# Moving per-head and closing arithmetic of a two-layer graph attention kernel from VectorE to GpSimd

## The chip, the core and the metric

The kernel runs on one core of a Trainium2 chip. The metric is the device time of one execution in microseconds (us). The core has five engines that run their own instruction streams and meet only in semaphores: TensorE (PE in the profile; its weight loads are listed apart as PEld), VectorE (DVE), ScalarE (ACT), GpSimd (POOL) and SyncE (SP, which here only issues DMAs). Kernels are compared by the median of several executions of each on the same chip.

## What is computed

Two graph attention layers over 4096 nodes with 128 features, each followed by a residual sum and a layernorm. `adj` is a 4096 x 4096 matrix of 0 and 1. Layer 0 has four heads of width 32, layer 1 has one head of width 128:

```python
# layer 0, for each head h (W: 128x128, a: 1x4x64)
Wh = (h @ W).reshape(N, H, D)
s_src = jnp.einsum('nhd,hd->nh', Wh, a_src)
s_dst = jnp.einsum('nhd,hd->nh', Wh, a_dst)
e = s_src[:, None, :] + s_dst[None, :, :]
e = jnp.where(e >= 0, e, ALPHA * e)
e = jnp.where(adj[:, :, None] > 0, e, NEG_INF)
attention = jax.nn.softmax(e, axis=1)
h_prime = jnp.einsum('ijh,jhd->ihd', attention, Wh)
return jax.nn.elu(h_prime.reshape(N, H * D))
# around the layers
x = _layernorm(x + _L0_gnn_ref(x, adj, L0_gnn_W, L0_gnn_a), axis=-1)
x = _layernorm(x + _L1_gnn_ref(x, adj, L1_gnn_a), axis=-1)
```

Layer 1 does the same with one head on a logarithmic map of the rows, and maps its result back.

## The kernel before, in words

The exponential of a leaky ReLU of a sum falls into two products, one for pairs whose sum is positive ("above") and one for the others ("below"). So a head is two matrix products of 0/1 masks with weighted values, and the masks are all that depends on the pair. This is what the engines do for layer 0:

- The 4096 target rows are cut into four chunks (`NC` = 4, counter `c`) of 1024 columns. A chunk has four heads, a head eight units, so `U` = 32 units per chunk (counter `u`, `UH` = 8 per head). A unit covers four source tiles of 128 nodes.
- A unit's comparison is made by ScalarE (four `Sign` activations, L620) or by VectorE (four `tensor_scalar`, L633), as the table `ON_ACT` says, letter A or V. VectorE then ANDs it with the adjacency mask (L653 after ScalarE, L657 after itself), which gives the "below" mask. A unit marked `-` in the table `DIRECT` gets a second VectorE instruction, an XOR (L663), for the "above" mask. A unit marked D has no XOR: TensorE multiplies the whole adjacency mask instead, with the below mask taking part in both column groups, so its 64 matmuls (L688) are 32 of 99 columns and 32 of 198 columns, against 64 of 99.
- Masks pass to TensorE through `ring`: six slots for below masks and two for above masks. VectorE waits before an XOR until an above slot is free.
- After a head, `take_head` sums the four accumulator banks out of PSUM (L704, four `tensor_reduce`; they free the banks for the next head) and then does the head's arithmetic in SBUF: scale by `lift` (L708), subtract (L709), reciprocal (L712), divide (L713). It stands behind unit `u % 8 == 1` of the next head (`TAKE_AT` = 1).
- After a chunk's last head, ScalarE takes an exponential for the ELU (`elu_exp`, L721, at u = 4 of the next chunk), and VectorE closes the chunk in five pieces behind units 3, 4, 5, 6 and 11 (`PIECES_AT`): `hidden_sum` (L466, L468), `moments` (L473), `centre` (L479 to L482), and two times `dot` (multiply L488 and row sum L489).
- Meanwhile TensorE transposes the next chunk's adjacency (L536), eight transposes to a group and sixteen groups to a chunk, ScalarE takes them (L543), and GpSimd issues the loads of adjacency tiles (`load_adj`, L501). Issuing DMAs is all that GpSimd does from 9 us on.
- In the last chunk VectorE and ScalarE also begin with layer 1: square roots, logarithms and exponentials of the rows that are already closed, then its weighted values (L731 to L752).
- Layer 1 then runs over eight runs of 512 rows (matmuls L1277, L1299, L1289), with the comparisons on ScalarE (L767).

The order of every engine's work is written out by hand: each engine has its own loop over `c` and `u`, and what stands behind which unit is given by numbers such as `TAKE_AT`.

## Time and profile before

| | us |
|---|---|
| median of 3 runs | 916.73 (915.87 to 918.69) |
| the profiled execution, its own time | 914.89 |
| its span, first to last instruction | 913.1 |
| PE busy | 839.0 |
| DVE busy | 761.4 |
| ACT busy | 694.4 |
| POOL busy | 43.0 |

Busy time is the time in which an engine works on at least one instruction; loads, waits and semaphore instructions are not in it. The granted TensorE clock over the span is 0.976 of full speed. Layer 0's units run from about 77 us to 541 us, layer 1's matmuls from 580 us to the end. In the chain of work that ended last, TensorE has 50% of the span, ScalarE 24% and VectorE 18%.

### The profile page before, as it was taken

How to read it: one execution, taken by the hardware profiler on the slowest of the kernel's cores; microseconds unless marked ns; L12 is line 12 of the kernel's file. 1: busy time of each engine (PE TensorE's matmuls, PEld its weight loads, DVE VectorE, ACT ScalarE, POOL GpSimd, SP SyncE). 2: the span in 40 equal slices, each digit the busy share in tenths (PEclk: the TensorE clock that was granted, in tenths of full speed). 3: DMA queues.
4: the chain of work that ended last, by engine and by line, in shares of the span. 5: the costliest groups of instructions: out<-in, count | busy, mean ns of one | idle time of the engine just before them, and what ended most of it. 6: DMA issues, size and time to landing. Idle time of an engine off the chain costs nothing.

```text
span 913.1 us, 24394 instructions
## 1 busy us (share of the span) xinstructions
PE 839.0 (92%) x10868; PEld 686.8 (75%) x10868; DVE 761.4 (83%) x1306; ACT 694.4 (76%) x815; POOL 43.0 (5%) x80
## 2 busy tenths in 40 slices
PE   8496999989999889999998898599999999999995
PEld 6496999978999879999998884355555555555552
DVE  3978889899988999889997889775877786878876
ACT  3999998897999989999986994968373654637222
POOL 3200000000000000000000000000000100000000
PEclk9799999999999999999999999799999999999998
DMA  8999377703658227113040002430324453644000
GB/s 146 177 106 249 54 86 77 233 25 35 85 71 197 84 25 86 34 69 143 25 118 19 7 27 68 70 104 13 104 86 159 137 177 104 198 129 153 2 12 14
DMA packets 42065, 84.67 MB, mean 93 GB/s; under 512 B 6242, under 2 KB 31332, under 8 KB 41316
## 3 DMA queue, kind: packets, MB, share of 16 engines
q0 software_dynamic: 12416, 33.56, 26.3%
q1 hardware_dynamic: 29540, 49.50, 15.1%
q8 instruction: 87, 1.43, 0.7%
q14 instruction: 22, 0.18, 0.1%
HBM read 112.27 MB, written 21.12 MB: 146 GB/s over the span
## 4 chain that ended last, share of the span: by engine, by line
PE 50%; ACT 24%; DVE 18%; issue 3%; DMA 3%; POOL 1%; SPq 0%; DVEq 0%; ACTq 0%
PE bank L1299 21%; PE bank L688 18%; ACT ring L620 16%; PE bank L1277 7%; ACT masks L767 3%; DVE ring L653 3%; DVE ring L633 3%; DMA adj_tiles<-in_adj_dram 3%; PE bank L1289 2%; PE bank L536 2%; ACT masks L523 1%; DVE evac L704 1%; DVE ring L657 1%; DVE ring L663 1%; ACT moving L573 1%
## 5 line engine op out<-in xcount | busy, mean ns | idle before, releaser
L688 PE MATMUL bank<-moving,ring 128*128 128x99 bf16 (+1 forms) x6528 | 451.9, 218 | 12.2 <-DVE ring L663 8.8
L688 PEld LDWEIGHTS bank<-moving,ring 128*128 128x128 fp8e4 x6528 | 388.2, 98 | 14.3 <-DVE ring L663 10.0
L620 ACT ACTIVATE ring<-s_rows,scores 128x1024 fp8e4<-128x1024 f32 x372 | 393.1, 1141 | 4.4 <-PE bank L688 3.7
L688 PE MATMUL bank<-moving,masks 128*128 128x99 bf16 x1664 | 222.7, 209 | 18.3 <-DVE evac L704 14.7
L688 PEld LDWEIGHTS bank<-moving,masks 128*128 128x128 fp8e4 x1664 | 163.1, 98 | 20.3 <-DVE ring L657 9.1
L1299 PE MATMUL bank<-moving,masks 128*128 128x387 bf16 x1056 | 178.2, 327 | 0.0
L767 ACT ACTIVATE masks<-s_rows,adj_tiles 128x512 fp8e4<-128x512 f32 x256 | 157.8, 709 | 0.1
L1299 PEld LDWEIGHTS bank<-moving,masks 128*128 128x128 fp8e4 x1056 | 101.7, 96 | 73.0
L653 DVE SCALAR_TENSOR_TENSOR ring<-ring,masks 128x1024 int32<-128x1024 int32 x93 | 113.1, 1217 | 10.9 <-ACT ring L620 10.8
L663 DVE TENSOR_TENSOR ring<-masks,ring 128x1024 int32<-128x1024 int32 x76 | 93.1, 1225 | 26.9 <-PE bank L688 25.2
L395 ACT ACTIVATE ring<-ring 128x4 f32<-128x4 f32 (+1 forms) x24 | 4.9, 205 | 141.0 <-DVE ring L311 115.3
L633 DVE TENSOR_SCALAR ring<-s_rows,neg_d 128x1024 uint8<-128x1024 f32 x140 | 96.0, 750 | 0.0
L1277 PE MATMUL bank<-moving,masks 128*128 128x387 bf16 x384 | 66.8, 337 | 13.0 <-DVE masks L783 13.0
L780 DVE SCALAR_TENSOR_TENSOR masks<-masks 128x1024 int32<-128x1024 int32 x32 | 39.2, 1224 | 37.9 <-ACT masks L767 37.9
L1277 PEld LDWEIGHTS bank<-moving,masks 128*128 128x128 fp8e4 x384 | 37.9, 99 | 41.5 <-DVE masks L783 13.4
L1299 PE MATMUL bank<-adj_tiles,masks 128*128 128x387 bf16 x352 | 62.2, 328 | 0.5 <-DVE ring L791 0.5
L543 ACT ACTIVATE masks<-bank 128x1024 uint16<-128x1024 uint16 x48 | 48.3, 1013 | 10.3 <-PE bank L536 9.3
L1299 PEld LDWEIGHTS bank<-adj_tiles,masks 128*128 128x128 fp8e4 x352 | 34.4, 98 | 24.9 <-DVE ring L791 0.9
L791 DVE TENSOR_REDUCE ring<-bank 128x129 f32<-128x387 f32 x60 | 29.4, 550 | 22.2 <-PE bank L1299 17.7
L657 DVE TENSOR_TENSOR ring<-ring,masks 128x1024 int32<-128x1024 int32 x35 | 42.6, 1217 | 0.0
L783 DVE TENSOR_TENSOR masks<-masks 128x1024 int32<-128x1024 int32 x32 | 39.2, 1224 | 1.1
L704 DVE TENSOR_REDUCE evac<-bank 128x132 f32<-128x396 f32 x64 | 31.9, 558 | 0.0
(214 smaller groups left out, 630.7 us busy)
## 6 DMA issues: line engine op xcount, KB each, us to landing
masks_kept<-masks SPq DMA_DIRECT2D x4, 4096.0 KB, 17.2
masks<-masks_kept SPq DMA_DIRECT2D x8, 2048.0 KB, 9.9
adj_tiles<-in_adj_dram POOLq DMA_DIRECT2D x24, 512.0 KB, 8.5
s_rows<-score_rows SPq DMA_DIRECT2D x14, 512.0 KB, 4.8
ring<-masks_kept POOLq DMA_DIRECT2D x11, 512.0 KB, 3.9
first_part<-masks_kept POOLq DMA_DIRECT2D x11, 512.0 KB, 3.8
second_part<-masks_kept POOLq DMA_DIRECT2D x10, 512.0 KB, 4.0
adj_tiles<-in_adj_dram POOLq DMA_DIRECT2D x16, 256.0 KB, 14.1
```

What stands on the lines that cost most here:

```text
L543: act.activation(dst[:, j:j + GQ, t * P:(t + 1) * P], turn_bank[q % 4][:, :].bitcast(U16).rearrange("p (j i) -> p j i", i=P), ACT.Copy, bi ...
L620: last = act.activation(j_tile(below, k), s_rows[:, h % 2, :], ACT.Sign, bias=scores[:, g * JU + k, h:h + 1], saturate=False)
L633: last = dve.tensor_scalar(j_tile(below, k), s_rows[:, h % 2, :], neg_d[:, h, j:j + 1], float(TWO), ALU.is_lt, ALU.mult)
L653: dve.scalar_tensor_tensor(out=below, in0=below, scalar=1, in1=m, op0=ALU.logical_shift_right, op1=ALU.bitwise_and).then_inc(done, 1)
L657: dve.tensor_tensor(below, below, m, ALU.bitwise_and).then_inc(done, 1)
L663: dve.tensor_tensor(above_slot(c, u).bitcast(I32), m, below, ALU.bitwise_xor).then_inc(unit_ready, 1)
L688: last = pe.matmul(bank[b][:, at + lo:at + hi], mask, moving[:, j, h, lo:hi], start=first, stop=(j == T - 1), skip_group_check=True)
L704: dve.tensor_reduce(evac[:, 2 * b:2 * b + 2, :, :].rearrange("p t b k -> p (t b) k"), parts, axis=AXX, op=ALU.add).then_inc(acc_taken, 1)
L767: last = act.activation(j_tile1(sides_of_run[y][1], j), s_rows1[:, y, :], ACT.Sign, bias=d1[:, j:j + 1], saturate=False)
L780: dve.scalar_tensor_tensor(out=mine, in0=mine, scalar=1, in1=here, op0=ALU.logical_shift_right, op1=ALU.bitwise_and).then_inc(below1_ready, 1)
L1277: last = pe.matmul(bank[2 * t + side][:, 0:PARTS * K1].rearrange("p (q k) -> p q k", q=PARTS), j_tile1(sides_of_run[e][side], j)[:, t * P: ...
L1299: last = pe.matmul(bank[2 * t + side][:, 0:PARTS * K1].rearrange("p (q k) -> p q k", q=PARTS), j_tile1(sides_of_run[e % 2][side], j)[:, t ...
```

## The change

GpSimd gets the arithmetic that follows VectorE's sums, and VectorE gets more of the masks.

- `take_head` is split. `take_banks` (the four sums out of PSUM) stays on VectorE, and so does the reciprocal, now called `invert`, behind unit `u % 8 == 2`. The scaling, the subtraction, the `empties` comparison of head 0 and the division are `divide_head` on GpSimd. Only the very last head of the last chunk is divided on VectorE.
- Of a chunk's closing, the hidden sum (now four instructions: min, add, max, add), the centring and the two multiplications by the attention vectors go to GpSimd for the first three chunks. VectorE keeps the moments, the means and the two row sums, at units 11, 12, 15 and 17. The ELU's exponential on ScalarE moves from unit 4 to unit 7. The last chunk is closed on VectorE as before.
- New semaphores hand the data over: VectorE's next sums wait until GpSimd has used `evac` (`mixed_taken`), the reciprocal waits for the subtraction, GpSimd's division waits for the reciprocal (`inverted`), and each step of the closing waits for the one before it on the other engine.
- GpSimd's adjacency loads are now issued inside its loop over the units, between the arithmetic.
- `ON_ACT`: five units go from ScalarE to VectorE, two each in chunks 1 and 2 and one in chunk 3. `DIRECT`: ten units lose their D, four each in chunks 1 and 2 and two in chunk 3.
- The early work of layer 1 in the last chunk stands one or two units later.

```diff
-              "AVAAVAAA" "AVAAVAAA" "AVAAVAAA" "AVAAVAAA"
-              "AVAAVAAA" "AVAAVAAA" "AVAAVAAA" "AVAAVAAA"
-              "AVAAVAAA" "AVAAVAAA" "AVAAVAAA" "AAAAVAAA"]
+              "AVAVAAVA" "AVAAVAAA" "AVAVAAVA" "AVAAVAAA"
+              "AVAVAAVA" "AVAAVAAA" "AVAVAAVA" "AVAAVAAA"
+              "AVAVAAVA" "AVAAVAAA" "AVAAVAAA" "AAAAVAAA"]
...
-              "DD------" "DD------" "DD------" "DD------"
-              "DD------" "DD------" "DD------" "DD------"
-              "DD-DD-D-" "DD-DD-D-" "DD-DD-D-" "DD-D-D--"]
+              "D-------" "D-------" "D-------" "D-------"
+              "D-------" "D-------" "D-------" "D-------"
+              "DD-DD-D-" "DD-D--D-" "DD-D--D-" "DD-D-D--"]
...
-    PIECES_AT = [3, 4, 5, 6, 11, 13]
+    PIECES_AT = [11, 12, 15, 17]
...
+        def hidden_on_pool(step, c):
+            step.engine.wait_ge(elu_given, c + 1)
+            flat = lambda ap: ap.rearrange("p t f -> p (t f)")
+            mine = feat[:, c * CT:(c + 1) * CT, :]
+            pool = step.engine
+            step(pool.tensor_scalar(flat(work), flat(work), 1.0, None, ALU.min))
+            step(pool.tensor_tensor(flat(work), flat(work), flat(mine), ALU.add))
+            step(pool.tensor_scalar(flat(attended), flat(attended), 0.0, None, ALU.max))
+            pool.tensor_tensor(flat(work), flat(attended), flat(work), ALU.add).then_inc(hidden_ready, 1)
+            pool.wait_ge(hidden_ready, c + 1)
+
+        def centre_on_pool(step, c):
+            pool = step.engine
+            pool.wait_ge(moments_ready, c + 1)
+            step(pool.tensor_tensor(feat[:, c * CT:(c + 1) * CT, :], work, mean_var[:, :, 0:1].broadcast_to([P, CT, F]),
+                                    ALU.subtract))
+
+        def weigh_dot_on_pool(step, c, k):
+            pool = step.engine
+            if k == 1:
+                pool.wait_ge(dot_summed, 2 * c + 1)
+            a = a1_spread[:, k:k + 1, :].broadcast_to([P, CT, F])
+            pool.tensor_tensor(work, feat[:, c * CT:(c + 1) * CT, :], a, ALU.mult).then_inc(dot_weighed, 1)
...
-        def take_head(step, c, h):
-
-            dve = step.engine
+        def take_banks(dve, c, h):
+
+            if c * H + h > 0:
+                dve.wait_ge(mixed_taken, c * H + h)
...
+        def invert(dve, c, h):
+            dve.wait_ge(mixed_taken, c * H + h + 1)
+            dve.reciprocal(inverse[:, :], mixed[:, :, D]).then_inc(inverted, 1)
...
+            step(engine.tensor_tensor(evac[:, :, 0, :], evac[:, :, 0, :], over(lift[:, h, mine], CT, K0), ALU.mult))
+            engine.tensor_tensor(mixed[:, :, :], evac[:, :, 1, :], evac[:, :, 0, :], ALU.subtract).then_inc(mixed_taken, 1)
+            engine.wait_ge(mixed_taken, c * H + h + 1)
...
+                engine.wait_ge(inverted, c * H + h + 1)
+            last = engine.tensor_tensor(attended[:, :, h * D:(h + 1) * D], mixed[:, :, 0:D], over(inverse[:, :], CT, D),
+                                        ALU.mult)
...
+                for c in range(NC):
+                    for u in range(U):
+                        if u % UH == TAKE_AT and u > UH:
+                            divide_head(step, c, u // UH - 1)
+                        if c > 0:
+                            if u == TAKE_AT:
+                                divide_head(step, c - 1, H - 1)
+                            if u == 7:
+                                hidden_on_pool(step, c - 1)
+                            if u == 12:
+                                centre_on_pool(step, c - 1)
+                                weigh_dot_on_pool(step, c - 1, 0)
+                            if u == 14:
+                                weigh_dot_on_pool(step, c - 1, 1)
...
-                        if c > 0 and u == 4:
+                        if c > 0 and u == 7:
                             elu_exp(act, c - 1)
...
-                take_head(step, NC - 1, H - 1)
+                take_banks(dve, NC - 1, H - 1)
+                dve.wait_ge(heads_divided, 1)
+                divide_head(step, NC - 1, H - 1)
```

## Rows read from the trace of the kernel before

**Rows 1.** Windows: us, then busy (count) by engine, clock, DMA share, GB/s.

```profile
88.99:170.83 81.84, 81.23 (x1529) 80.99 (x1527) 71.51 (x86) 76.05 (x75) 4.60 (x8) 1.00 0.66 90
170.83:291.61 120.78, 113.14 (x2181) 111.57 (x2178) 111.08 (x147) 111.32 (x110) 4.60 (x8) 0.99 0.51 89
291.61:410.79 119.18, 111.39 (x2181) 110.14 (x2178) 111.09 (x147) 116.10 (x114) 2.12 (x4) 1.00 0.34 75
410.79:486.12 75.33, 72.75 (x1270) 72.38 (x1267) 73.64 (x132) 65.00 (x65) 0.00 (x0) 1.00 0.26 87
486.12:541.48 55.36, 49.12 (x823) 48.56 (x820) 41.98 (x51) 54.84 (x59) 0.00 (x0) 0.94 0.04 11
```

**Rows 2.** Chain that ended last: start us, us, what; ACT and TensorE units.

```profile
243.19 8.32 ACT ring L620 x8
...
343.24 2.91 PE bank L688 x64
...
392.98 4.13 PE bank L688 x64
```

**Rows 3.** Waits: who waited for whom, us in total, times, longest.

```profile
DVE ring L663 <- PE bank L688: 25.2, 26, 3.2
```

**Rows 4.** Timeline of DVE, start of chunk 1: start us, us, what.

```profile
177.78 0.43 DVE L708 TENSOR_TENSOR evac<-evac,lift 128x264 f32<-128x264 f32 x1
...
178.72 0.20 DVE L712 RECIPROCAL inverse<-mixed 128x8 f32<-128x8 f32 x1
178.95 0.42 DVE L713 TENSOR_TENSOR first_part<-mixed,inverse 128x256 f32<-128x256 f32 x1
179.29 1.22 DVE L653 SCALAR_TENSOR_TENSOR ring<-ring,masks 128x1024 int32<-128x1024 int32 x1
...
181.69 2.74 DVE L633 TENSOR_SCALAR ring<-s_rows,neg_d 128x1024 uint8<-128x1024 f32 x4
184.34 1.22 DVE L653 SCALAR_TENSOR_TENSOR ring<-ring,masks 128x1024 int32<-128x1024 int32 x1
185.59 1.22 DVE L663 TENSOR_TENSOR ring<-masks,ring 128x1024 int32<-128x1024 int32 x1
186.74 1.22 DVE L466 SCALAR_TENSOR_TENSOR second_part<-second_part,feat 128x1024 f32<-128x1024 f32 x1
...
189.13 1.22 DVE L657 TENSOR_TENSOR ring<-ring,masks 128x1024 int32<-128x1024 int32 x1
```

**Rows 5.** Timeline of POOL, the program's start.

```profile
0.25 0.10 POOL L1591 MEMSET const-float32-0.0<- 128x1 f32 x1 [0.25 <-issue]
...
0.89 0.20 POOL L1173 MEMSET ident<- 128x128 f32 x1
...
1.68 0.28 POOL L1178 CAST ident_b<-ident 128x128 bf16<-128x128 f32 x1
```

**Rows 6.** Timeline of POOL: three of its DMA issues.

```profile
26.64 2.85 POOL L497 DMA_DIRECT2D adj_tiles<-in_adj_dram  x4 [11.48 <-PE bank L514]
...
105.94 0.53 POOL L501 DMA_DIRECT2D adj_tiles<-in_adj_dram  x1 [38.12 <-PE bank L536]
...
274.09 0.89 POOL L501 DMA_DIRECT2D adj_tiles<-in_adj_dram  x1 [10.81 <-PE bank L536]
```

**Rows 7.** DVE beside those issues: one line's durations, then two timeline rows.

```profile
L633 DVE TENSOR_SCALAR ring<-s_rows,neg_d x1: 952/952/952, 29.0 to 29.0; 128x1024 uint8<-128x1024 f32 x1
...
105.30 1.23 DVE L663 TENSOR_TENSOR ring<-masks,ring 128x1024 int32<-128x1024 int32 x1 [1.31 <-PE bank L688]
...
274.12 0.75 DVE L633 TENSOR_SCALAR ring<-s_rows,neg_d 128x1024 uint8<-128x1024 f32 x1
```

**Rows 8.** Groups by line: sums (L704), two inputs (L488), one (L489).

```profile
L704 DVE TENSOR_REDUCE evac<-bank 128x132 f32<-128x396 f32 x64 | 31.9, 558 | 0.0
...
L489 DVE TENSOR_REDUCE dots<-second_part 128x8 f32<-128x1024 f32 x8 | 9.8, 1220 | 0.3
L488 DVE TENSOR_TENSOR second_part<-feat,a_spread 128x1024 f32<-128x1024 f32 x8 | 9.7, 1217 | 0.0
```

More of the change, by code:

```diff
@@ L489, in dot, with moments_of, means_of, sum_dot @@
             return step.post(dve.reduce_sum(dots[:, k, c * CT:(c + 1) * CT], work, axis=AXX))
+        def hidden_on_pool(step, c):
[19 more added lines that the diff above has]
+            pool.tensor_tensor(work, feat[:, c * CT:(c + 1) * CT, :], a, ALU.mult).then_inc(dot_weighed, 1)
+        def moments_of(step, c):
+            dve = step.engine
+            dve.wait_ge(hidden_ready, c + 1)
+            for t in range(CT):
+                last = dve.bn_stats(stats[:, t, 0:6], work[:, t, :])
+            return step.post(last)
+        def means_of(step, c):
+            dve = step.engine
+            for t in range(CT):
+                last = dve.bn_aggr(mean_var[:, t, :], stats[:, t, 0:6])
+            last.then_inc(moments_ready, 1)
+            dve.wait_ge(moments_ready, c + 1)
+            dve.tensor_copy(var[:, c * CT:(c + 1) * CT], mean_var[:, :, 1])
+        def sum_dot(dve, c, k):
+            dve.wait_ge(dot_weighed, 2 * c + k + 1)
+            dve.reduce_sum(dots[:, k, c * CT:(c + 1) * CT], work, axis=AXX).then_inc(dot_summed, 1)
         fast_closing = Closing("close", inv_std=inv_std, **fast_close)
@@ L716, in take_head @@
             else:
-                step.post(last)
+                step(last)
         def elu_exp(act, c):
@@ L1185, in _ @@
                     load_quarter(pool, k)
-                for c in range(1, NC):
-                    for t in range(CT):
-                        if c == 1 and t < AHEAD:
-                            pool.wait_ge(turned, (QUARTERS - 1 + t // 2) * (Q // QUARTERS))
-                        else:
-                            pool.wait_ge(turned, c * Q + (t - AHEAD + 1) * QT)
-                        load_adj(pool, c, t)
+                step = Chain(pool, pool_steps)
+                for t in range(AHEAD):
+                    pool.wait_ge(turned, (QUARTERS - 1 + t // 2) * (Q // QUARTERS))
+                    load_adj(pool, 1, t)
+                for c in range(NC):
[12 more added lines that the diff above has]
+                                weigh_dot_on_pool(step, c - 1, 1)
+                        for q in groups_at(c, u):
+                            t = q // QT
+                            if q % QT == QT - 1 and t + AHEAD < CT:
+                                pool.wait_ge(turned, (c + 1) * Q + (t + 1) * QT)
+                                load_adj(pool, c + 1, t + AHEAD)
+                            elif q % QT == QT - 1 and c + 2 < NC:
+                                pool.wait_ge(turned, (c + 1) * Q + (t + 1) * QT)
+                                load_adj(pool, c + 2, t + AHEAD - CT)
+                pool.sem_inc(heads_divided, 1)
                 pool.wait_ge(unit_done, NC * U)
@@ L1460, in _, with piece @@
                 summed_at = [0]
+                def piece(c, n):
+                    if n == 0:
+                        summed_at[0] = moments_of(step, c)
+                    elif n == 1:
+                        step.need(summed_at[0])
+                        means_of(step, c)
+                    else:
+                        sum_dot(dve, c, n - 2)
                 def late_weights(n):
@@ L1475, in _ @@
                         if u % UH == TAKE_AT and u > UH:
-                            take_head(step, c, u // UH - 1)
+                            take_banks(dve, c, u // UH - 1)
+                        if u % UH == TAKE_AT + 1 and u > UH:
+                            invert(dve, c, u // UH - 1)
                         if c == 0:
```

42 lines of the change are left out of this document (25 added, 17 removed).

## The prediction

> **What bounds the kernel now.** I read the windows first, one for each chunk of layer 0 [rows 1]. The reader should see that no single engine bounds it: in chunk 1 (170.83 to 291.61, 120.8 us) TensorE is busy 113.1, ScalarE 111.3 and VectorE 111.1 us; in chunk 2 (119.2 us) ScalarE leads with 116.1, and VectorE and TensorE have 111. Chunk 3 has two halves. Up to 486.12 VectorE is busy 73.6 of 75.3 us, and after it ScalarE 54.8 of 55.4 us while VectorE has 42.0. Chunk 0 from 88.99 on is TensorE's (81.2 of 81.8), with VectorE idle for 10.3 us. Then the chain that ended last, for the price of one unit on each engine [rows 2]: ScalarE compares two units in 8.32 us, 4.16 each; TensorE needs 2.91 us for a unit of two masks and 4.13 for a direct one, so a D costs it 1.22 us. The waits show how tight the coupling is [rows 3]: VectorE waits 25.2 us in 26 places for TensorE to free an above slot. So a microsecond taken from one engine alone is worth little, and one added to VectorE in chunks 1 to 3a is soon paid in full: its idle time is 9.7, 8.1 and 1.7 us there.
>
> **The change part by part.** Prices of VectorE are start-to-start times [rows 4].
>
> Head arithmetic leaves VectorE: L708 and L709 run from 177.78 to 178.72, 0.94 us, and L713 holds the engine from 178.95 to 179.29, 0.34. That is 1.28 us a head, for 15 heads, 19.2 us. The reciprocal stays.
>
> Closing leaves VectorE: the hidden sum from 186.74 to 189.13, 2.39 us; the centring and two multiplications are of the same size (one op from 186.74 on is about 1.2), 3.6. Together 6.0 us a chunk, 18.0 us for three.
>
> Masks come to VectorE: a compared unit is 2.65 us (181.69 to 184.34), five of them 13.3. A unit that loses its D gets an XOR: 184.34 to 186.74 is 2.40 us for both operations, against 1.15 for one such operation alone (185.59 to 186.74), so 1.25 each and 12.5 us for ten. ScalarE loses 5 x 4.16 = 20.8 us, TensorE 10 x 1.22 = 12.2 us.
>
> On VectorE's own account: chunks 1 and 2 each lose 4 x 1.28 + 6.0 = 11.1 and gain 2 x 2.65 + 4 x 1.25 = 10.3, so -0.8 each. Chunk 3 up to 486 loses 2 x 1.28 + 6.0 = 8.6 and gains 2.65 + 1.25 = 3.9, so -4.7. Its second half loses 2.6 and gains 1.25. Chunk 0 loses 3.8. What is freed on VectorE is thus nearly all spent again; the relief is on the other two engines.
>
> GpSimd's new work has no row. Its nearest rows are small ones [rows 5]: a memset of one element a partition takes 0.10 us, of 128 elements 0.20, and a cast of 128 elements, which also reads, 0.28. So a step costs about 0.10 us plus 0.8 ns an element when it only writes and 1.4 ns when it reads one input. An instruction with two inputs lies between 1.4 ns (the second costs nothing) and 2.8 ns (it costs the same again). For 264 elements that is 0.47 to 0.84 us, for 1024 elements 1.5 to 3.0; for min and max over 1024 elements with one input 0.9 to 1.5. I take the middles, 0.65, 2.25 and 1.2, since nothing stands nearer to one end. A head is three steps, 1.95 us (1.4 to 2.5). A closing is two one-input and five two-input steps, 2.4 + 11.25 = 13.65 us (9.3 to 18). A chunk: 4 x 1.95 + 13.65 = 21.5 us (15 to 28), all of layer 0 some 70 us on an engine that has 43 busy now. If it runs freely it is hidden: 21.5 of 120 us. The Trainium skill gives a price of its own ("GPSIMD Engine Reference", section 3.1): 4497 ns for a two-input add over 2048 elements. By it 1024 elements would be an estimated 2.3 us, and the sum would stay as it is.
>
> **Does it run freely?** This is the term that decides. Two of VectorE's rows say how many inputs it can stream [rows 8]: a reduction with one input of 1024 elements takes 1.220 us, a multiplication with two such inputs 1.217. So it has two read paths, and the second input uses the second. A comparison (L633) reads one input of 1024 elements in 0.75 us, faster than one path gives, so it uses both as well. And comparisons are just what is seen to collide with GpSimd: the DMA issue at 274.09 takes 0.89 instead of 0.53 us beside the comparison at 274.12 [rows 6, 7], and the comparison at 29.03, begun while the issues of 26.64 to 29.49 were running, takes 0.952 instead of 0.75. The issue at 105.94 keeps its 0.53 us beside an XOR (105.30 to 106.53). An issue writes but doesn't read, so this last row doesn't clear the XOR of colliding with GpSimd arithmetic that reads. I take it that one of VectorE's paths is also GpSimd's, and that comparisons, ANDs, XORs and every two-input step exclude GpSimd's arithmetic and are excluded by it. Only VectorE's sums out of PSUM (31.9 us for four chunks, 8.0 each) and the row sums (2 x 1.22) run beside it [rows 8]: 10.4 us a chunk, with the statistics about a tenth of its time.
>
> The Trainium skill states the same as a rule ("SBUF — State Buffer", section "SBUF: two separate sides"): the shared pair of ports is an exclusive lock for a whole instruction, and VectorE wants it in a two-port mode or, against a GpSimd instruction that reads SBUF, with two SBUF inputs. The two rows on comparisons agree; no row here shows the second half. By the rule 70 us of arithmetic would stop VectorE for as long.
>
> Then GpSimd's time adds to VectorE's. Chunk 1: 111.1 - 0.8 + 21.5 = 131.8 us, less a tenth of the 21.5 that falls beside sums, 129.7, against a span of 120.8: +8.9. Chunk 2: the same 129.7 against 119.2: +10.5. Chunk 3 up to 486: 73.6 - 4.7 + (2 x 1.95 + 13.65) = 86.5, less 1.8, 84.7 against 75.3: +9.4. Its second half: 42.0 - 1.4 + 3.9 = 44.5 of 55.4, hidden under ScalarE. Chunk 0: 3 x (1.95 - 1.28) = +2.0 against 10.3 idle, nothing. Sum +28.8 us. The profiled execution would go from 914.9 to 943.7; the median is 1.8 higher, so 945.5. With GpSimd's lower price (15 a chunk) it is about 17 us less, 929; with the upper one 18 more, 963. TensorE and ScalarE get idle time instead of a gain.
>
> **New waits.** VectorE's reciprocal behind unit 2 waits for GpSimd's subtraction, and ANDs and XORs of unit 3 are queued behind it, with TensorE behind them. GpSimd has one unit (3.7 us) for 1.3 us of work, but at u = 10 the hidden sum (about 7 us from u = 7 on) lies in front of it. If it isn't done, VectorE waits, but while it waits GpSimd runs alone, so most of it is time already counted: 0 to 2 us a chunk, taken as nothing. VectorE's sums wait for `mixed_taken` of the head before, eight units old: free. ScalarE's exponential at u = 7 waits for a division due at u = 1: free. The adjacency loads stand behind arithmetic in GpSimd's queue and could be late by one closing step, but a tile is loaded four tiles ahead (four times about 10 us): free. The last head waits for `heads_divided`, long given. Layer 1's early work one or two units later falls in the half that ScalarE bounds: 0 to +1.
>
> **The rivals.**
> (a) GpSimd arithmetic disturbs nobody. Then the busiest engine counts. Chunk 1: VectorE 110.3, TensorE 113.1 - 4.9 = 108.2, ScalarE 103. The span exceeded the busiest engine by 7.7 before, so about 118: -3. Chunk 2: ScalarE 107.8, VectorE 110.3; 3 to 8 over it, about 116: -4. Chunk 3 up to 486: VectorE 68.9, TensorE 71.5, so about 73: -2. Second half: ScalarE loses nothing there; 0 to -2. Sum -10 (-4 to -17): 907. For it speaks that no row shows VectorE held up by a GpSimd instruction that reads; against it the stretched comparison.
> (b) Only comparisons exclude it. They are 10 x 2.65 of 110 us in a chunk, a quarter, so 5 of the 21.5 us come on top: chunk 1 at 115.5 plus 5 to 8 of coupling is where it was, and the others too. Time 912 to 921, about 916. For it speaks the undisturbed XOR beside the issue.
> (c) They exclude each other, but VectorE always goes first and GpSimd takes the gaps. Idle time is about 10 us a chunk against 21.5 of work, so GpSimd comes late and VectorE waits at its reciprocals and sums; 10 us a chunk come back as waits less what overlaps, 925 to 940. This lies in the forecast's direction and within its range.
> The slower side is the forecast itself; the faster rival (a) is decided by one thing, whether a two-input VectorE instruction beside GpSimd arithmetic keeps its 1.22 us.
>
> **How the numbers follow.** Exclusion, in the full form or as (c), 0.55, range 925 to 963; (a) 0.32, 900 to 913; (b) 0.13, half of it within the 0.3% of 916.7 (2.8 us), about what a measurement of this kernel can tell from no change. Slower 0.57, same 0.10, faster 0.33. The predicted time is that of the likeliest, 945. For 8 in 10 the range must take in most of (a), and it leaves out only its lower end and the upper price of GpSimd: 902 to 957. The forecast's own range is 925 to 963.
>
> **What would show it.** Right: in the profile after, L653, L657 and L663 have maxima well over 1.22 us, up to that plus a GpSimd step, where POOL is busy; VectorE is busy nearly all of chunks 1, 2 and 3a; ScalarE and TensorE idle more than before; chunk 1 is longer than 120.8 us. Wrong: two-input instructions keep 1.22 us beside POOL (rival a), or only L633 grows (b), or GpSimd's steps are the long ones and VectorE waits at L712's successor (c). Steps of GpSimd under 1.5 or over 3.0 us for 1024 elements would shift the sum by the ends given.

## The result and the profile after

| | before | after |
|---|---|---|
| median, us | 916.30 (914.98 to 918.69, 4 runs) | 947.71 (945.59 to 949.19, 4 runs) |
| the profiled execution, its span | 914.89, 913.1 | 946.88, 945.0 |
| busy: PE, DVE, ACT, POOL | 839.0, 761.4, 694.4, 43.0 | 842.2, 798.4, 675.3, 161.0 |

The change makes the kernel slower by 3.4%: the ratio is 1.034, with a 95% interval of 1.031 to 1.037. The forecast was 945 us, in the direction that it gave 57%.

The windows of the kernel after, one for each chunk (chunk 0 from 89 us on, 1, 2, and the two parts of 3), answer to [rows 1]. Each chunk is cut where VectorE starts its first comparison, and chunk 3 once more where VectorE ends the AND of its unit 19, as before. The columns are the same, with busy time in the order PE, PEld, DVE, ACT, POOL:

```profile
89.00:171.10 82.10, 81.49 (x1533) 81.25 (x1531) 71.19 (x79) 76.31 (x75) 14.73 (x17) 1.00 0.65 85
171.10:302.75 131.65, 113.88 (x2181) 112.00 (x2178) 125.00 (x140) 105.59 (x104) 40.08 (x28) 0.92 0.46 80
302.75:435.79 133.04, 114.33 (x2189) 112.63 (x2186) 124.91 (x141) 108.63 (x107) 37.33 (x24) 0.92 0.32 77
435.79:519.98 84.19, 73.08 (x1246) 72.38 (x1243) 82.34 (x122) 63.20 (x63) 31.78 (x17) 0.94 0.20 69
519.98:573.57 53.59, 49.30 (x851) 47.72 (x849) 42.97 (x49) 50.67 (x55) 4.13 (x3) 0.97 0.05 12
```

Chunk 0 is 0.3 us longer than before, chunk 1 10.9, chunk 2 13.9, the first part of chunk 3 8.9, and its second part is 1.8 shorter. The sum is 32.1 us, and the span grew by 31.9: the whole loss lies in layer 0 from 171 us on. VectorE is busy 125 of 132 us in chunk 1, and the granted TensorE clock is 0.92 where it was 0.99.

The next view gives for one line all durations of an instruction: minimum, median and maximum in ns. L679, L699, L703 and L709 were L633, L653, L657 and L663; L751 and L535 are the sums of [rows 8]:

```profile
L679 DVE TENSOR_SCALAR ring<-s_rows,neg_d x160: 708/748/2854, 29.2 to 556.3; 128x1024 uint8<-128x1024 f32 x160
L699 DVE SCALAR_TENSOR_TENSOR ring<-ring,masks x88: 1208/1217/3371, 37.9 to 568.6; 128x1024 int32<-128x1024 int32 x88
L703 DVE TENSOR_TENSOR ring<-ring,masks x40: 1176/1215/2057, 34.3 to 560.4; 128x1024 int32<-128x1024 int32 x40
L709 DVE TENSOR_TENSOR ring<-masks,ring x86: 1224/1226/3278, 92.5 to 569.9; 128x1024 int32<-128x1024 int32 x86
L751 DVE TENSOR_REDUCE evac<-bank x64: 553/558/565, 85.8 to 577.4; 128x132 f32<-128x396 f32 x64
L535 DVE TENSOR_REDUCE dots<-second_part x6: 1207/1209/1212, 240.4 to 510.2; 128x8 f32<-128x1024 f32 x6
```

All four mask instructions have maxima of 2.1 to 3.4 us over medians that haven't moved, and the two reductions never stretch. The groups by line give the size: mean durations of 880, 1351, 1229 and 1404 ns, against 748 to 1226 undisturbed, make 160 x 0.131 + 88 x 0.134 + 40 x 0.012 + 86 x 0.179 = 48.6 us of stretching.

How it happens is seen in the timelines of VectorE and of GpSimd over the hidden sum in chunk 1 (start, duration, what), where [rows 4] showed the same instructions at 1.22 and 2.74:

```profile
190.27 4.29 DVE L679 TENSOR_SCALAR ring<-s_rows,neg_d 128x1024 uint8<-128x1024 f32 x4
194.48 3.36 DVE L699 SCALAR_TENSOR_TENSOR ring<-ring,masks 128x1024 int32<-128x1024 int32 x1
197.88 1.94 DVE L709 TENSOR_TENSOR ring<-masks,ring 128x1024 int32<-128x1024 int32 x1
199.74 1.21 DVE L703 TENSOR_TENSOR ring<-ring,masks 128x1024 int32<-128x1024 int32 x1
200.98 3.26 DVE L709 TENSOR_TENSOR ring<-masks,ring 128x1024 int32<-128x1024 int32 x1
...
218.08 0.20 DVE L756 RECIPROCAL inverse<-mixed 128x8 f32<-128x8 f32 x1 [0.64 <-POOL mixed L767]
```

```profile
190.75 3.27 POOL L499 TENSOR_SCALAR second_part<-second_part 128x1024 f32<-128x1024 f32 x1 [3.87 <-ACT second_part L784]
194.10 2.66 POOL L500 TENSOR_TENSOR second_part<-second_part,feat 128x1024 f32<-128x1024 f32 x1
196.85 3.62 POOL L501 TENSOR_SCALAR first_part<-first_part 128x1024 f32<-128x1024 f32 x1
200.55 2.61 POOL L502 TENSOR_TENSOR second_part<-first_part,second_part 128x1024 f32<-128x1024 f32 x1
```

The AND at 194.48 takes 3.36 us beside a two-input addition of 2.66 us (194.10 to 196.76), and the XOR at 200.98 takes 3.26 beside that of 200.55. Each ends 1.1 us after GpSimd's addition has ended, which is about its own undisturbed time. So here the two engines take turns. Beside the one-input `min` and `max` (L499, L501) the comparisons grow from 2.74 to 4.29 and an XOR to 1.94, which is much less than GpSimd's 3.27 and 3.62.

Two places of the chain that ended last, and the waits (who waited for whom: us, times, longest), answer to [rows 2, 3]:

```profile
234.57 4.64 PE bank L734 x64
...
331.53 5.53 PE bank L734 x64
```

```profile
PE bank L734 <- DVE evac L751: 31.9, 13, 8.5
...
ACT ring L666 <- PE bank L734: 28.6, 10, 6.5
...
DVE ring L709 <- PE bank L734: 21.3, 19, 3.4
```

A unit of two masks took TensorE 2.91 us, and these two take 4.64 and 5.53 us. The windows over exactly these two units give the granted clock in them, 0.63 and 0.50:

```profile
234.57:239.21 4.64, 4.64 (x68) 4.64 (x69) 3.43 (x3) 4.58 (x5) 0.00 (x0) 0.63 0.06 23
331.53:337.06 5.53, 5.53 (x67) 5.53 (x68) 5.47 (x3) 0.00 (x0) 3.21 (x2) 0.50 0.11 41
```

The second runs at the lower of TensorE's two clock levels throughout, 1.2 instead of 2.4 GHz, and takes nearly twice as long. In the chain, a stretched AND and a stretched XOR stand before each of them (2.87 and 3.29 us before the first, 3.29 and 1.95 before the second).

TensorE waits 31.9 us for VectorE's sums (14.7 before, in 9 places), and ScalarE's signs wait 28.6 us for TensorE to free a slot (3.7 before). Back at the hidden sum, the window of the 6 us in which VectorE does the stretched AND and XOR, and the one after it, show the granted clock where TensorE runs out of masks:

```profile
195.00:201.00 6.00, 1.13 (x14) 1.13 (x15) 5.93 (x4) 3.98 (x4) 5.82 (x3) 0.68 0.26 86
201.00:207.00 6.00, 6.00 (x105) 6.00 (x103) 5.96 (x4) 2.14 (x3) 2.16 (x1) 0.75 0.01 4
```

TensorE works 1.13 of 6 us for lack of masks. When it has masks again, the granted clock is 0.75: for a part of that stretch it runs at the lower level.

GpSimd's groups by line (us busy, mean ns) give the prices for which [rows 5] had only small instructions:

```profile
L516 POOL TENSOR_TENSOR second_part<-feat,a_spread 128x1024 f32<-128x1024 f32 x6 | 18.0, 3007 | 22.6 <-DVE dots L535 22.3
...
L501 POOL TENSOR_SCALAR first_part<-first_part 128x1024 f32<-128x1024 f32 x3 | 11.2, 3743 | 0.3
```

These durations include GpSimd's own waiting for its turn. All its arithmetic in layer 0 is about 118 us (161.0 busy less 43.0 before).

### The profile page after: what moved, and what is told of

It is laid out like the page before. It is cut to its first block, busy times and chain, and to the rows that moved or that the text cites. A ratio compares the mean times of both kernels' runs of the same rounds, so it can differ in the third digit from the quotient of the medians.

```text
span 945.0 us, 24465 instructions
## 1 busy us (share of the span) xinstructions
PE 842.2 (89%) x10868; PEld 688.3 (73%) x10868; DVE 798.4 (84%) x1272; ACT 675.3 (71%) x795; POOL 161.0 (17%) x150
## 4 chain that ended last, share of the span: by engine, by line
PE 55%; DVE 22%; ACT 13%; issue 5%; DMA 3%; POOL 2%; SPq 0%; DVEq 0%; PEldq 0%; ACTq 0%
PE bank L734 23%; PE bank L1382 20%; PE bank L1360 7%; ACT ring L666 6%; DVE ring L679 5%; DVE ring L699 3%; ACT masks L830 3%; DVE ring L709 3%; DMA adj_tiles<-in_adj_dram 2%; PE bank L1372 2%; DVE evac L751 2%; DVE ring L703 2%; PE bank L582 2%; ACT masks L569 1%; ACT moving L619 1%
## 5 line engine op out<-in xcount | busy, mean ns | idle before, releaser
L734 PEld LDWEIGHTS bank<-moving,ring 128*128 128x128 fp8e4 x6848 | 397.8, 100 | 24.6 <-DVE ring L709 19.2
L666 ACT ACTIVATE ring<-s_rows,scores 128x1024 fp8e4<-128x1024 f32 x352 | 373.1, 1141 | 30.6 <-PE bank L734 28.6
L734 PE MATMUL bank<-moving,masks 128*128 128x99 bf16 x1344 | 187.1, 212 | 36.9 <-DVE evac L751 31.9
L734 PEld LDWEIGHTS bank<-moving,masks 128*128 128x128 fp8e4 x1344 | 134.4, 100 | 39.7 <-DVE ring L709 17.3
L1382 PEld LDWEIGHTS bank<-moving,masks 128*128 128x128 fp8e4 x1056 | 101.7, 96 | 73.0
L709 DVE TENSOR_TENSOR ring<-masks,ring 128x1024 int32<-128x1024 int32 x86 | 120.7, 1404 | 23.7 <-PE bank L734 21.3
L679 DVE TENSOR_SCALAR ring<-s_rows,neg_d 128x1024 uint8<-128x1024 f32 x160 | 130.6, 880 | 0.0
L699 DVE SCALAR_TENSOR_TENSOR ring<-ring,masks 128x1024 int32<-128x1024 int32 x88 | 118.8, 1351 | 8.4 <-ACT ring L666 8.3
L589 ACT ACTIVATE masks<-bank 128x1024 uint16<-128x1024 uint16 x48 | 48.6, 1014 | 32.9 <-PE bank L582 31.9
L843 DVE SCALAR_TENSOR_TENSOR masks<-masks 128x1024 int32<-128x1024 int32 x32 | 39.2, 1224 | 38.1 <-ACT masks L830 38.1
L1360 PEld LDWEIGHTS bank<-moving,masks 128*128 128x128 fp8e4 x384 | 37.8, 99 | 41.2 <-DVE masks L846 13.4
L703 DVE TENSOR_TENSOR ring<-ring,masks 128x1024 int32<-128x1024 int32 x40 | 49.1, 1229 | 0.0
L766 POOL TENSOR_TENSOR evac<-evac,lift 128x264 f32<-128x264 f32 x15 | 17.4, 1158 | 177.8 <-DVE evac L751 172.9
```

What stands on the lines that cost most here:

```text
L589: act.activation(dst[:, j:j + GQ, t * P:(t + 1) * P], turn_bank[q % 4][:, :].bitcast(U16).rearrange("p (j i) -> p j i", i=P), ACT.Copy, bi ...
L666: last = act.activation(j_tile(below, k), s_rows[:, h % 2, :], ACT.Sign, bias=scores[:, g * JU + k, h:h + 1], saturate=False)
L679: last = dve.tensor_scalar(j_tile(below, k), s_rows[:, h % 2, :], neg_d[:, h, j:j + 1], float(TWO), ALU.is_lt, ALU.mult)
L699: dve.scalar_tensor_tensor(out=below, in0=below, scalar=1, in1=m, op0=ALU.logical_shift_right, op1=ALU.bitwise_and).then_inc(done, 1)
L703: dve.tensor_tensor(below, below, m, ALU.bitwise_and).then_inc(done, 1)
L709: dve.tensor_tensor(above_slot(c, u).bitcast(I32), m, below, ALU.bitwise_xor).then_inc(unit_ready, 1)
```

## The experiments

My theory was that of the prediction: GpSimd's arithmetic and VectorE's mask work exclude each other. Against it stood that the handovers or the queues cost the time, that only comparisons are touched, or that the new tables do the harm.

**One half at a time.** The first kernel keeps the new work of GpSimd and takes back both tables:

```diff
-              "AVAVAAVA" "AVAAVAAA" "AVAVAAVA" "AVAAVAAA"
+              "AVAAVAAA" "AVAAVAAA" "AVAAVAAA" "AVAAVAAA"
...
-              "D-------" "D-------" "D-------" "D-------"
+              "DD------" "DD------" "DD------" "DD------"
```

> The changed kernel with the two tables (who compares, which units are direct) of the kernel before; GpSimd still does the head arithmetic and the closing. Theory (exclusion: a two-input or comparing VectorE instruction and a GpSimd arithmetic instruction shut each other out): VectorE loses 10.3 us of masks in chunks 1 and 2 each and 3.9 in chunk 3, is busy about 115 us in chunk 1 (125.0 in the changed kernel), and the time falls to 920 to 932, still above the kernel before. Rival (the redistribution of masks is what cost the time, GpSimd's arithmetic is harmless): 917 or less. Rival (the new handshakes cost it, whatever is compared where): stays above 940.

Measured: 931.95 us against 914.65, ratio 1.019 (1.018 to 1.021). The second is the kernel before with only the new tables.

> The kernel before with only the two tables of the changed one; all arithmetic on VectorE, GpSimd only issues loads. Theory (exclusion): VectorE gets 10.3 us more in chunks 1 and 2 each and 3.9 in the first half of chunk 3 against idle times of 9.7, 8.1 and 1.7 us, so 3 to 8 us a chunk more: 925 to 940, clearly slower than before, and as much a part of the loss as the exclusion. Rival (the tables are a gain that GpSimd's arithmetic hides): 916 or less. No comparison or AND is longer than in the kernel before.

Measured: 930.54 us, ratio 1.018 (1.016 to 1.020). None of its mask instructions is stretched: the ANDs take at most 1.23 us, and the XORs' mean is as before:

```profile
L663 DVE TENSOR_TENSOR ring<-masks,ring 128x1024 int32<-128x1024 int32 x86 | 105.4, 1225 | 20.1 <-PE bank L688 17.8
```

So each half costs by itself, 17.3 and 15.9 us, and the sum of 33.2 is about what both cost together (31.4). The tables alone put 5 x 2.65 + 10 x 1.25 = 25.8 us on VectorE. They cost 15.9 although they relieve ScalarE and TensorE, which fits VectorE's 19.5 us of idle time in chunks 1 to 3a: it can absorb a part only. In chunk 1 of this run (172.59 to 297.68) VectorE is busy 121.4 of 125.1 us, and the granted clock is 0.95, although GpSimd does no arithmetic.

**The handovers without the arithmetic.** The third kernel is the one after, with GpSimd's instructions cut to 8 elements a partition. It leaves out most of the ELU, the hidden sum, the centring, the attention products and the division; ScalarE copies the features in place of the ELU's exponential, the exponents of layer 1 are scaled by 0.01, and its flag is held at 0.

```diff
-            flat = lambda ap: ap.rearrange("p t f -> p (t f)")
+            flat = lambda ap: ap.rearrange("p t f -> p (t f)")[:, 0:8]
...
-            pool.tensor_tensor(work, feat[:, c * CT:(c + 1) * CT, :], a, ALU.mult).then_inc(dot_weighed, 1)
+            pool.tensor_tensor(work[:, 0, 0:8], feat[:, c * CT, 0:8], a1_spread[:, k, 0:8], ALU.mult).then_inc(dot_weighed, 1)
```

> The changed kernel with all its handshakes and tables, but each GpSimd arithmetic instruction of layer 0 works on 8 elements a partition instead of 264 or 1024, so the division of the heads and the hidden sums, centring and products of the first three chunks are left out (ScalarE copies x where it took the exponential of the attended values, layer 1's exponents are scaled by 0.01, and the flag for the general path is held at 0). Theory (exclusion): VectorE's instructions are back at 1.22 us, and the time is that of rival (a) of the prediction, 900 to 913, about 907. Rival (the handshakes, or the longer waits behind them, cost the time): stays above 930. Rival (neither: the masks alone are too much for VectorE): about 925.

Measured: 907.89 us, ratio 0.992 (0.990 to 0.994). Its window over chunk 1, cut as above, and the group of its XORs:

```profile
171.99:287.88 115.89, 107.79 (x2181) 106.51 (x2178) 109.84 (x140) 105.13 (x104) 20.64 (x27) 0.99 0.52 87
```

```profile
L708 DVE TENSOR_TENSOR ring<-masks,ring 128x1024 int32<-128x1024 int32 x86 | 105.4, 1225 | 34.1 <-PE bank L733 32.0
```

All semaphores, queue orders and tables of the change are in it, and it is faster than the kernel before. So the handovers as such cost nothing, and the new tables fit into VectorE's time once its own arithmetic is gone. What this kernel leaves out as well is waiting behind long GpSimd steps. In the kernel after, VectorE's reciprocals wait 3.2 us for that in all, in 5 places.

Chunk 1 can be compared directly, since tables and matmuls are the same. It takes 115.89 us here and 131.65 in the kernel after. VectorE is busy 109.84 us here and 125.00 there, and idle for 6.05 and 6.65. So of the 15.8 us between them 15.2 are longer instructions of VectorE. TensorE is busy 107.79 us at a clock of 0.99, and 113.88 at 0.92 in the kernel after.

**The price of exclusion, by itself.** The fourth kernel computes nothing of the reference, and was run once. VectorE and GpSimd run in phases, 16 independent instructions of VectorE (XOR, comparison or row sum) beside 4 of GpSimd, each of which waits for the one before it:

```python
phases = [(d, p) for d in (None, xor, compare, reduce) for p in (None, two, short, scalar, write) if d or p]
```

> No attention is computed: x is copied to the output, and beside it runs a grid of phases, 16 independent VectorE instructions of one kind next to 4 chained GpSimd instructions of one kind. VectorE: none, XOR of two int32 inputs, comparison of one f32 input, sum of one f32 input, all of 1024 elements. GpSimd: none, add of 1024 elements, add of 264, min of one input of 1024, memset of 1024. Theory (exclusion): adds and mins stretch XORs and comparisons, so that a phase lasts as long as VectorE's 16 alone (18 to 20 us, 11 for comparisons) plus GpSimd's 4 alone (each add 1.9 to 2.8 us, 8 to 11 in all); the sums keep 1.22 us and their phases last as long as the longer of the two. The memset, which reads nothing, stretches comparisons but not XORs. Rival (only comparisons exclude GpSimd): XOR phases last as long as the longer side. Rival (VectorE always goes first): VectorE's 16 keep their time and GpSimd's run after them.

First its timeline with GpSimd alone: additions of 1024 and of 264 elements, `min` of 1024, and a memset of 1024. Then its windows, with DVE and POOL busy time: five phases of XORs (alone, then beside each kind in that order), five of comparisons, and the row sums alone and beside the addition of 1024.

```profile
6.38 9.59 POOL L37 TENSOR_TENSOR pc<-pa,pb 128x1024 f32<-128x1024 f32 x4 [2.92 <-DVEq L66]
16.15 3.19 POOL L40 TENSOR_TENSOR pc<-pa,pb 128x264 f32<-128x264 f32 x4 [0.18 <-DVEq L66]
19.55 11.31 POOL L43 TENSOR_SCALAR pc<-pa 128x1024 f32<-128x1024 f32 x4 [0.21 <-DVEq L66]
31.02 3.98 POOL L46 MEMSET pc<- 128x1024 f32 x4 [0.15 <-DVEq L66]
```

```profile
35.08:53.48 18.40, 18.26 (x16) 0.00 (x0) 1.00 0.00 0
53.48:80.45 26.97, 26.83 (x16) 13.03 (x4) 1.00 0.00 0
80.45:101.08 20.63, 20.47 (x16) 5.54 (x5) 1.00 0.00 0
101.08:122.86 21.78, 21.65 (x16) 11.85 (x5) 1.00 0.00 0
122.86:141.29 18.43, 18.25 (x16) 3.80 (x4) 1.00 0.00 0
141.29:152.12 10.83, 10.69 (x16) 0.00 (x0) 1.00 0.00 0
152.12:171.34 19.22, 19.07 (x16) 10.34 (x5) 1.00 0.00 0
171.34:184.17 12.83, 12.67 (x16) 3.95 (x5) 1.00 0.00 1
184.17:201.20 17.03, 16.91 (x16) 13.47 (x5) 1.00 0.00 0
201.20:215.09 13.89, 13.71 (x16) 5.08 (x4) 1.00 0.00 0
215.09:233.35 18.26, 18.12 (x16) 0.00 (x0) 1.00 0.00 0
233.35:251.60 18.25, 18.11 (x16) 9.39 (x4) 1.00 0.00 0
```

The phase's length less that of VectorE alone, over four, is what one GpSimd instruction costs VectorE:

| GpSimd instruction | alone, us | costs XORs | costs comparisons | costs row sums |
|---|---|---|---|---|
| add, 1024 | 2.40 | 2.14 | 2.10 | 0.00 |
| add, 264 | 0.80 | 0.56 | 0.50 | - |
| min, 1024 | 2.83 | 0.85 | 1.55 | - |
| memset, 1024 | 1.00 | 0.01 | 0.77 | - |

A two-input step of 1024 elements on GpSimd costs VectorE's XORs and comparisons nearly its whole length, one of 264 elements about two thirds of it. The probe has no AND. On VectorE the same step costs 1.2 us (1024 elements) or 0.43 (264) [rows 4]. Moving it away is thus a loss for VectorE as long as it does XORs or comparisons meanwhile: 0.9 us for the long one, 0.1 for the short one.

**Heads alone, closing alone.** The fifth kernel is the one before with only the head arithmetic on GpSimd; its closing stays on VectorE, but at units 7, 8, 10, 11 and 13, with the exponential at 6. The sixth has only the closing on GpSimd, with the exponential and the hidden sum at unit 4. Like the first kernel it keeps the later places of the pieces and of layer 1's early work from the kernel after. One line of the fifth, against the kernel before:

```diff
-            step(dve.tensor_tensor(evac[:, :, 0, :], evac[:, :, 0, :], over(lift[:, h, mine], CT, K0), ALU.mult))
+            step(engine.tensor_tensor(evac[:, :, 0, :], evac[:, :, 0, :], over(lift[:, h, mine], CT, K0), ALU.mult))
```

> The kernel before (its tables too) with only the head arithmetic on GpSimd; the closing stays on VectorE, its pieces at units 7, 8, 10, 11 and 13 and the exponential at 6, since the division comes later. From the grid of phases a two-input GpSimd instruction of 264 elements costs VectorE (20.63 - 18.40) / 4 = 0.56 us among XORs and (12.83 - 10.83) / 4 = 0.50 among comparisons, so about 1.6 us a head, against 1.28 us that VectorE saves. Exclusion priced so: 0.3 us a head worse, 12 heads in bound chunks, with some waits at the reciprocal +3 to +8 us: 917 to 923. Rival (what costs is the handshake and not the exclusion): as much as in the changed kernel, over 925. Rival (small instructions are harmless): 914 or less.

Measured: 917.63 us against 915.04, ratio 1.0026 (1.0017 to 1.0036).

GpSimd's loop of the sixth, as it differs from the kernel before:

```diff
+                            if u == 4:
+                                hidden_on_pool(step, c - 1)
+                            if u == 12:
+                                centre_on_pool(step, c - 1)
+                                weigh_dot_on_pool(step, c - 1, 0)
+                            if u == 14:
+                                weigh_dot_on_pool(step, c - 1, 1)
```

> The changed kernel with the old tables and the head arithmetic back on VectorE: of GpSimd's new work only the closing of the first three chunks is left (exponential and hidden sum at unit 4). From the grid: a two-input instruction of 1024 elements costs VectorE (26.97 - 18.40) / 4 = 2.14 us among XORs, a one-input one (21.78 - 18.40) / 4 = 0.85 there and (17.03 - 10.83) / 4 = 1.55 among comparisons; five and two of them make about 13 us a chunk, against 6.0 saved. So +7 a chunk less what idle time takes in: 925 to 935. If heads and closing add up, the excess of this run and of the one with the heads only make 17 us together, that of both with the old tables. Rival (the heads with their 45 small instructions are the costly part): below 920.

Measured: 934.38 us, ratio 1.022 (1.019 to 1.025). The windows over chunk 1, first of the fifth kernel, then of the sixth:

```profile
172.23:291.93 119.70, 112.80 (x2181) 111.49 (x2178) 108.02 (x133) 112.57 (x111) 21.24 (x21) 0.99 0.52 89
172.23:296.15 123.92, 112.82 (x2181) 111.53 (x2178) 117.72 (x141) 113.63 (x112) 25.48 (x15) 0.99 0.48 84
```

The table above foresees the closing. It is five long two-input steps and two one-input steps, 5 x 2.14 + 2 x 0.85 (or 1.55) = 12.4 to 13.8 us. Without exclusion VectorE would be busy 111.08 - 6.0 = 105.1 us in chunk 1, and it is busy 117.72, so 12.6 were taken. Over three chunks, less the 6.0 relieved, the table gives 19 to 23 us, and the time rose by 19.3.

For the heads the table is too high. A head is three short steps, 3 x 0.56 = 1.7 us, and four heads 6.7. Without exclusion VectorE would be busy 111.08 - 4 x 1.28 = 106.0 us, and it is busy 108.02, so only 2.1 were taken. The time rose by 2.6. Why the short steps take so little from VectorE in the kernel was not tested.

The closing is the harm, the heads are nearly neutral. 12.6 and 2.1 make 14.7 us, just what VectorE is stretched by in chunk 1 of the kernel after (125.00 less 110.3), and near the 14.0 of the first kernel, which has both with the old tables (113.9 less 100.0). The two rises in time, 22 us, are more than the 17.3 of both together; the placement of the pieces differs between these kernels.

**The clock.** The four steps of the hidden sum run back to back for 12 us, and that is where TensorE starves. If the lower clock had a price of its own, steps set apart should cost less. I tried it with waits on TensorE's progress first, and the exponential at unit 5:

```diff
-                            if u == 7:
-                                hidden_on_pool(step, c - 1)
+                            if 5 <= u <= 8:
+                                pool.wait_ge(unit_done, c * U + u - 3)
+                                hidden_on_pool(step, c - 1, u - 5)
```

> The changed kernel, but the four GpSimd instructions of the hidden sum no longer follow one another: each waits for one more unit of TensorE (units 2 to 5 done), and ScalarE's exponential stands at unit 5. The same instructions exclude the same ones, so VectorE's stretched time stays near 48 us. In the changed kernel TensorE's granted clock is 0.92 in chunks 1 and 2 (0.99 and 1.00 before), with 0.68 in the 6 us in which these four run back to back. If those stretches of starvation and the slower clock after them add to the loss, the clock of both chunks rises and the time falls by 3 to 8 us, to 938 to 943. Rival (only the sum of the excluded time counts): 945 to 948 as the changed kernel, whatever the clock does.

Measured: 949.40 us against 916.16, ratio 1.037 (1.035 to 1.039). The time is above both ranges of the expectation. It says nothing on the question: the four steps started at 189.56, 193.25, 196.01 and 199.55, back to back as before, and the clock over chunk 1 is 0.94. The next kernel waits on VectorE's masks instead.

```diff
+                                pool.wait_ge(unit_ready, c * U + (4, 5, 7, 8)[u - 5])
```

> The run before on this question left the four instructions of the hidden sum back to back (they start at 189.56, 193.25, 196.01 and 199.55 us), since the units of TensorE that they waited for were done already. Here they wait for VectorE's masks of units 4, 5, 7 and 8 instead, so that at least one full unit of VectorE lies between the second and the third. If starving TensorE in one stretch, and the slower clock that follows, adds to the loss, then the granted clock of chunk 1 rises over 0.92 and the time falls by 3 to 8 us below the changed kernel's 947.7. Rival (only the sum of the excluded time counts): 945 to 950.

Its GpSimd timeline, and its window over chunk 1:

```profile
193.23 2.68 POOL L502 TENSOR_TENSOR second_part<-second_part,feat 128x1024 f32<-128x1024 f32 x1
203.09 3.25 POOL L504 TENSOR_SCALAR first_part<-first_part 128x1024 f32<-128x1024 f32 x1 [7.18 <-DVE ring L713]
207.22 2.74 POOL L506 TENSOR_TENSOR second_part<-first_part,second_part 128x1024 f32<-128x1024 f32 x1 [0.89 <-DVE ring L713]
```

```profile
171.00:303.00 132.00, 114.01 (x2178) 112.14 (x2176) 124.34 (x139) 105.43 (x103) 40.18 (x28) 0.94 0.47 81
```

Measured: 948.79 us against 915.61, ratio 1.035 (1.033 to 1.038). Now the second and third step are 7 us apart, but the clock in chunk 1 is only 0.94 instead of 0.92 and the time is that of the kernel after. Setting these steps apart won nothing, as the rival of the expectation said, but the clock hardly rose either. What the clock costs by itself stays open.

**A version that beats both.** In the kernel before, ScalarE is busy 54.8 of 55.4 us in the second half of chunk 3, and VectorE has 13 us idle there [rows 1]. So two of ScalarE's last units (22 and 25 of the chunk) go to VectorE:

```diff
-              "AVAAVAAA" "AVAAVAAA" "AVAAVAAA" "AAAAVAAA"]
+              "AVAAVAAA" "AVAAVAAA" "AVAAVAVA" "AVAAVAAA"]
```

> The kernel before with one edit: two units of the last chunk's second half (22 and 25) are compared by VectorE instead of ScalarE. There ScalarE is busy 54.8 of 55.4 us, TensorE 49.1 and VectorE 42.0. ScalarE loses 8.3 us, VectorE gains 5.3: TensorE is then the busiest. If that half is ScalarE's alone it gets 3 to 5 us shorter: 910 to 912 where before is 914.7. Rival (ScalarE's rounding of layer 1's weights and the waits around it set the pace there): less than 1 us.

Measured: 909.38 us against 915.04, ratio 0.994 (0.992 to 0.995).

> The kernel before with the two late units (22 and 25 of the last chunk) compared by VectorE, measured once more beside the other runs: 909 to 911 where before is 915 to 916, a ratio of 0.993 to 0.995.

Measured once more: 909.56 us against 915.61, again 0.994 (0.992 to 0.995). Window and chain of that run, over the stretch of the last row of [rows 1]:

```profile
486.12:541.48 55.36, 51.42 (x894) 50.74 (x891) 52.18 (x66) 51.49 (x58) 0.00 (x0) 0.97 0.04 12
```

```profile
489.93 21.43 PE bank L688 x351
...
517.13 8.32 ACT ring L620 x8
```

TensorE now sets 21 us of the half in which the chain had been ScalarE's from 486 to 536. Two further steps gave nothing more: unit 4 of the last chunk to ScalarE as well,

```diff
-              "AVAAVAAA" "AVAAVAAA" "AVAAVAVA" "AVAAVAAA"]
+              "AVAAAAAA" "AVAAVAAA" "AVAAVAVA" "AVAAVAAA"]
```

> As the run before, and one unit of the first half of the last chunk (4), where VectorE is busy 73.6 of 75.3 us and ScalarE 65.0, goes from VectorE to ScalarE. VectorE loses 2.65 us there, ScalarE gains 4.2, TensorE is busy 72.8: 1 to 2.5 us less than the run before, 908 to 911. Rival (TensorE, only 0.9 us behind VectorE, holds that half): no difference from the run before.

with 910.28 us (ratio 0.9945, 0.9932 to 0.9959), and a unit of chunk 2 to VectorE and direct,

```diff
-              "AVAAVAAA" "AVAAVAAA" "AVAAVAAA" "AVAAVAAA"
+              "AVAAVAAA" "AVAAVAAA" "AVAVAAVA" "AVAAVAAA"
...
-              "DD------" "DD------" "DD------" "DD------"
+              "DD------" "DD------" "DD-D----" "DD------"
```

> The kernel before with the two late units of the last chunk on VectorE, and in chunk 2, where ScalarE is busy 116.1 of 119.2 us and the other two 111, one more unit on VectorE (head 2, unit 3 of it), which is made direct as well. ScalarE loses 4.2 us there, VectorE gains 2.65 - 1.25, TensorE 1.2: 112 to 113 each. If the busiest engine sets the chunk: 1 to 3 us less than with the late units alone (909.4), 906 to 908. Rival (the coupling of three equally loaded engines costs what the leader gives back): 909 to 911.

with 911.30 us against 916.16 (0.9955, 0.9939 to 0.9971), just above its rival's 909 to 911. In chunk 2 ScalarE had led with 116.1 us against 111 for the others, and still the chunk takes 120.4 us here (291.80 to 412.16), with ScalarE busy 115.0, and 119.2 in the repeated run of the first edit (291.95 to 411.12). A lead of one engine alone doesn't promise a gain.

## Why the prediction came out

**What bounds the kernel: right in the main.** That time added to VectorE is soon paid was borne out by the tables alone: 25.8 us added, 15.9 paid. So was the reading that chunk 3's second half is ScalarE's: the only experiment that won time worked there.

**Exclusion: right, in kind and place.** The stretched masks, the undisturbed sums (L751, L535) and the 907.89 us without arithmetic say the same. That this is the 907 of rival (a) is partly luck: (a) had 10 us less than before, and 6.8 less were measured beside a kernel before at 914.65. Rival (b) is out, since XORs beside additions are stretched as much as comparisons (2.14 and 2.10 us). Rival (c) is out, since VectorE is held up in the middle of its instructions, and its reciprocals wait only 3.2 us in all.

The rule of the Trainium skill that the prediction weighed ("SBUF — State Buffer", section "SBUF: two separate sides") is borne out in the half that no row had shown: an XOR with two inputs loses 2.14 us to a GpSimd addition, which reads, and 0.01 to a memset, which doesn't. That the lock holds for a whole instruction is not what the runs show for `min`, which reads too: XORs lose 0.85 us to one of 2.83 us. There the measurement decides.

**GpSimd's prices: two right, one outside its bounds.** 264 elements cost 0.80 us (taken 0.65, bounds 0.47 to 0.84), two inputs of 1024 2.40 (taken 2.25, bounds 1.5 to 3.0). The one-input `min` costs 2.83, where I took 1.2 and allowed 0.9 to 1.5. The slope of a 128-element cast doesn't carry over to it. By the measured prices a chunk's arithmetic is 12 x 0.80 + 5 x 2.40 + 2 x 2.83 = 27.3 us and not 21.5. In chunk 1 of the kernel after GpSimd is busy 35.5 us more than before, its waiting for VectorE included.

**The stretch: too large, by the heads.** I charged VectorE with 90% of GpSimd's time, 19.4 us in chunk 1. Its busy time rose to 125.0 where 111.1 - 0.8 = 110.3 stood without exclusion, so the stretch was 14.7 us. For the closing 12.3 us were charged and 12.6 measured, for the four heads 7.0 and 2.1, measured in the kernels that have one of the two alone. The closing's term holds although its `min` and `max` were mis-priced, because these steps take only 0.85 to 1.55 us of their length from VectorE.

**The idle time: put at nothing, and wrong.** The sum let VectorE run without a gap in chunks 1, 2 and 3a, and took the new waits as nothing. In chunk 1 it is idle for 131.65 - 125.00 = 6.65 us, 5.1 of them until TensorE frees an above slot and 1.3 at reciprocals. In chunk 2 it is 8.1 us, in 3a 1.9.

Exclusion or a slow clock isn't needed for most of it. Without GpSimd's long steps it is 6.05 us in chunk 1, at a clock of 0.99, and 5.7 of them are again waits for above slots. With the new tables alone it is 3.7, and it was 9.7 in the kernel before. So some coupling to TensorE through the two above slots is in every version. The prediction had named it [rows 3] and then left it out of its sum.

**TensorE's clock: not in the prediction.** TensorE should have had 113.1 - 4.9 = 108.2 us of work in chunk 1. It has 107.79 at a clock of 0.99 without GpSimd's arithmetic, and 113.88 at 0.92 with it. So the same matmuls take 6.1 us more, and that goes with the clock. How much of it reaches the total is not shown.

**The total: right, partly by errors that cancel.** In chunk 1 the stretch was 4.7 us too high and the idle time 6.65 too low, which gives +8.9 forecast and +10.9 measured. Chunk 2 was put at +10.5 and is +13.9. Chunk 3 up to unit 19 was put at +9.4 and is +8.9; there VectorE is busy 82.3 us where 84.7 were forecast, and idle for 1.9 where nothing was. The second part of chunk 3 was put at nothing and is 1.8 us shorter. Together +28.8 were forecast and +31.9 measured. That the median came within 3 us is luck in part.

**The handovers and the queue order: right.** Taken at nothing. All of them are in the kernel that takes 907.89 us, and the waits behind long GpSimd steps, which are not, are the 3.2 us at the reciprocals.

## What to carry to other kernels

Before work is moved from VectorE to GpSimd, look at what VectorE runs meanwhile. Beside two-input or comparing instructions a two-input GpSimd step of 1024 elements took away 2.1 us of VectorE for a step that VectorE does in 1.2, and beside sums with one input it took nothing. Short steps were about neutral (15 heads cost 2.6 us). When several engines are busy within 10% of each other, try a unit or two in a stretch where one of them leads and another has room, rather than rebalance everywhere: two letters of a table gave 6 us, where the whole change lost 31. Measure each such move: of the three places tried here one gave something.

## What the hardware showed that I had not expected

- A one-input `min` on GpSimd is slower than a two-input addition of the same 1024 elements, 2.83 against 2.40 us, but takes far less from VectorE: 0.85 us from XORs, 1.55 from comparisons.
- A memset of 1.00 us on GpSimd costs comparisons 0.77 us and XORs nothing.
- GpSimd's head steps over 8 elements still took 0.72 to 0.77 us each in the mean, and its closing steps over 8 elements 0.55 to 1.21, and yet no XOR grew (1224 to 1228 ns over all 86). So most of that length is not time in which they exclude VectorE.
- TensorE's granted clock was 0.68 over a stretch in which it worked 1.13 of 6 us for lack of masks, and 0.75 over the next 6 us, in which it was busy throughout. A unit of 2.91 us took 5.53 at a clock of 0.50.
